# A nucleus-selection kernel whose repair branch sorts ties from real failures before it repeats

## What is computed

```python
Q = Xa @ W1; K = Xa @ W3
logits = Q @ W2 @ K.T / TAU
idx = jnp.argsort(-logits, axis=1)
vals = jnp.take_along_axis(logits, idx, axis=1)
csum = jnp.cumsum(jax.nn.softmax(vals, axis=1), axis=1)
k_i = jnp.sum(csum < P_NUC, axis=1) + 1          # P_NUC = 0.9
keep = jnp.take_along_axis(jnp.arange(n)[None, :] < k_i[:, None], jnp.argsort(idx, axis=1), axis=1)
A = jax.nn.softmax(jnp.where(keep, logits, -jnp.inf), axis=1)
...
for s in range(STEPS):                            # STEPS = 2
    A = _adj_from_feats(Xa, W1, W2, W3)
    Xf = Rf @ Xf; Xb = Rb @ Xb; Xa = A @ Xa
    Z = Z + (Xf @ U1[s] + Xb @ U2[s] + Xa @ U3[s])
```

## Time and profile before

| | us |
|---|---|
| median of 3 runs | 2081.41 |
| lowest, highest | 2080.66, 2081.58 |
| the execution that was profiled | 2080.55 |
| its span, first to last instruction | 2078.9 |
| mean granted TensorE clock | 0.951 of full speed |

### The profile page before, as it was taken

How to read it: one execution, slowest core, us unless ns; L and a number is a source line. 1 busy time by engine, 2 the same in 40 slices (tenths; PEclk the granted TensorE clock), 3 DMA queues, 4 the chain that set the end, 5 groups by cost and what they waited for, 6 DMA issues and landing times.

```text
span 2078.9 us, 37636 instructions
## 1 busy us (share of the span) xinstructions
PE 1784.7 (86%) x11660; PEld 1314.5 (63%) x11660; DVE 1667.7 (80%) x4213; ACT 1365.0 (66%) x2157; POOL 555.4 (27%) x869
## 2 busy tenths in 40 slices
PE   3999953899999999994765299999999999999997
PEld 2888831677777777773653166666666666666665
DVE  6444465899999999998851699999989999999996
ACT  5222266788888888884622586867676767677752
POOL 4000030343333333332230113131313232222220
PEclk9999976899999999997988699999999999999999
DMA  6999621444444444442333001010101010101022
GB/s 156 197 203 207 165 99 39 104 113 112 112 112 112 112 109 106 107 111 55 75 79 112 21 21 41 20 40 20 40 20 40 20 40 22 39 24 37 31 93 69
DMA packets 235346, 168.27 MB, mean 81 GB/s; under 512 B 188451, under 2 KB 220577, under 8 KB 235168
## 3 DMA queue, kind: packets, MB, share of 16 engines
q1 hardware_dynamic: 221264, 117.44, 20.8%
q0 software_dynamic: 3744, 22.14, 6.9%
q10 hardware_dynamic: 10288, 28.12, 4.0%
HBM read 107.99 MB, written 37.49 MB: 70 GB/s over the span
## 4 chain that ended last, share of the span: by engine, by line
DVE 46%; PE 18%; DVEq 17%; issue 11%; ACT 3%; DMA 3%; POOLq 0%; ACTq 0%; POOL 0%; SPq 0%
DVE probs_t L1508 7%; DVE stats L1525 5%; DVE stats L1515 5%; DVE window L1405 4%; DVEq L1706 4%; DVE scraps L1405 4%; DVE sorted_e L1534 2%; DVE window L1568 2%; DMA probs_t<-astray 2%; DVEq L1572 2%; DVE expo L1388 2%; DVEq L1532 2%; PE lg L1081 2%; PE bank L1029 2%; PE bank L1028 2%
## 5 line engine op out<-in xcount | busy, mean ns | idle before, releaser
L1081 PE MATMUL lg<-k_t,q_tile 64*128 64x512 f32 (+1 forms) x832 | 199.5, 582 | 134.3 <-DVE expo L1388 105.6
L1104 PE MATMUL bank<-both,s_tile 128*128 128x512 f16 x1352 | 300.1, 379 | 0.0
L1171 PE MATMUL bank<-xcur,probs_t 128*128 128x256 f32 x1352 | 296.1, 379 | 0.0
L1171 PEld LDWEIGHTS bank<-xcur,probs_t 128*128 128x128 f32 x1352 | 254.9, 190 | 33.6
L633 POOL TENSOR_TENSOR window<-window,probs_t 128x832 f16<-128x832 f32 x104 | 223.0, 2144 | 112.7 <-ACT probs_t L870 100.0
L1388 DVE TENSOR_SCALAR_CACHE_REDUCE expo<-lg 128x1024 f32 (+1 forms) x208 | 205.0, 1022 | 41.3 <-PE lg L1081 30.8
L1104 PEld LDWEIGHTS bank<-both,s_tile 128*128 128x128 bf16 x1352 | 132.3, 98 | 148.1
L1081 PEld LDWEIGHTS lg<-k_t,q_tile 64*128 64x128 f32 x832 | 72.2, 196 | 221.0 <-DVE expo L1388 134.3
L812 ACT ACTIVATE expo<-expo,neg_max 128x3327 f32<-128x3327 f32 x52 | 159.4, 3065 | 73.1 <-DVE neg_max L1397 73.1
L659 POOL TENSOR_TENSOR aims<-found 128x2 f32<-128x2 f32 x26 | 5.1, 194 | 649.0 <-ACT found L838 649.0
L833 ACT ACTIVATE turned<-expo,found 128x3327 uint8<-128x3327 f32 x52 | 159.7, 3071 | 3.6
(11 more groups left out here) (291 smaller groups left out, 3642.8 us busy)
## 6 DMA issues: line engine op xcount, KB each, us to landing
s_tile<-s_scratch SPq DMA_DIRECT2D x28, 832.0 KB, 4.5
expo<-in_adj POOLq DMA_DIRECT2D x25, 831.8 KB, 9.8
s_tile<-s_scratch ACTq DMA_DIRECT2D x24, 832.0 KB, 4.4
s_scratch<-s_tile SPq DMA_DIRECT2D x14, 832.0 KB, 9.8
s_scratch<-probs_t SPq DMA_DIRECT2D x6, 832.0 KB, 9.8
s_scratch<-window SPq DMA_DIRECT2D x6, 832.0 KB, 10.5
q_tile<-q_scratch SPq DMA_DIRECT2D x104, 32.0 KB, 2.1
xa_scratch<-ht ACTq DMA_DIRECT2D x26, 128.0 KB, 1.9
```

The lines of the kernel that those rows point to most:

```text
L1081: last = T.matmul(lg[c % 2][:, h * CHUNK:h * CHUNK + w], q_tile[b][DA * h:DA * (h + 1), :], k_all[DA * h:DA * (h + 1), s, c0:c0 + w], star ...
L1104: last = T.matmul(s_ps[:, 0:width], s_tile[b][:, k, :], moving, start=(k == 0 and part == 0), stop=(k == NT - 1 and part == 1))
L1171: last = T.matmul(kept_ps[1][:, 0:D], probs_t[:, k * P:(k + 1) * P], xcur[:, k, :], start=(k == 0), stop=(k == NT - 1))
```

## The change

Two things are done, both inside the repair branch.

First, in stage 0 alone, the test is taken again with ties allowed before the loop is entered: `tied` is taken out of `astray`, the list `equal` that `take_ties` needs is made, rows with more than 8 ties are put back, and `find_odd` and `reg_load` decide whether the loop runs at all. Secondly, in both stages, `take_ties` and `take_above` stand behind the loop, and are done once, instead of in each round.

```diff
                         dve.drain()
                         V.memset(tries, TRIES)
+                        if s == 0:
+                            V.tensor_tensor(astray[:, :], astray[:, :], tied, ALU.subtract)
+                            V.tensor_scalar(equal, ranks[:, :], tied, below[:, :], ALU.is_lt, ALU.mult)
+                            V.tensor_scalar(least, tied, 8.0, None, ALU.is_gt)
+                            dve.drain()
+                            V.tensor_tensor(astray[:, :], astray[:, :], least, ALU.add)
+                            dve.drain()
+                            find_odd(astray[:, :], t)
+                            dve.reg_load(left, odd_n[0:1, 0:1])
                         with dve.While(left):
                             move_cut(b)
                             rank(b)
                             flag(True)
                             dve.drain()
-                            take_ties(b)
-                            take_above(b, True, 0, N)
                             sum_kept()
                             find_odd(astray[:, :], t)
                             V.tensor_scalar(tries, tries, -1.0, None, ALU.add)
...
                             dve.reg_load(left, again)
+                        take_ties(b)
+                        take_above(b, True, 0, N)
+                        dve.drain()
                         dve.reg_load(left, odd_n[0:1, 0:1])
                         with dve.While(left):
                             climb(b)
```

## The result

The changed kernel took **2066.7 us** (median of 4 runs, 2066.2 to 2067.1) beside 2081.4 us of the kernel before on the same chip: a ratio of 0.993, 95% interval [0.9913, 0.9947]. So the change makes the kernel faster by 0.6 to 0.7%, 12 to 15 us. The forecast was 2068.8 us, 12.6 us less.

What follows compares the result with a forecast made beforehand. The prediction took DVE's two repair visits in stage 0 to lie on the path: -16.1 us in step 24 and +3.5 in step 22 make -12.6, from 2081.41 to 2068.8 us, range 2065.0 to 2074.5.

Steps and rivals of the forecast that it cites:

- What bounds it: Stage 0's repair branch, entered in steps 22 and 24, lies wholly on the path that sets the end.
- Which rows failed, and why: Step 22: row 1436's cut is too low, a true failure; step 24: row 1552 is only a tie.
- Rival 1: Step 24's row 1552 isn't a tie on the chip; the loop runs in both steps, +7.0 us, 2088.4 us; chance 0.05.
- rival 4: Both failures, steps 22 and 24, are ties, so 2 x 16.1 us go: 2049.2 us; chance 0.01.
- Step 24: Repair round skipped after the new test, masks kept; `kept_inv` at 1035.8 in place of 1051.89, 16.1 us earlier.
- Step 22: New test finds row 1436 and the loop runs: +3.2 us for the test, +0.3 for moved masks, +3.5 together.
- What is late next: After step 24's earlier `kept_inv`, ACT, POOL and PE still wait idle, margin 5.4 us on PE; gain passes in full.
- Rival 2: Step 24's gain is partly taken up in step 25 by a new wait, a third lost: 2074.2 us; chance 0.03.
- The sum: Whole kernel: -16.1 us in step 24 plus 3.5 in step 22 gives -12.6, so 2068.8 us.
- Stage 1 within 1 us: Sign to check: stage 1, untouched by the change, takes the same time as before to within 1 us.
- Rival 3: Stage 0's longer loop body makes each of 24 steps pay a 2.75 us jump, +66 us: 2134.8; chance 0.02.

Runs made afterwards that it cites:

- the cheaper test: Changed kernel with SyncE moving flag and `tied` per row and the entry test working on one partition instead of `find_odd`: 2066.4 us, ratio 0.9937; once more 2067.0.
- the filler runs: Changed kernel with 160, then 400 more instructions in the never-entered second loop of stage 0's repair branch: 2073.2 us (0.9967) and 2073.3 us (0.997).

## Why the prediction was right, point by point

- **What bounds it.** Both visits lie wholly on the path: a change of the branch's length by -27.5, +7.5 and +1.5 us in step 22, and by -27.4 and -15.3 us in step 24, came out at the end each time, within the spread of the runs. The -1.1 and -1.4 us of the cheaper test came as far as step 24's `kept_inv`, and are too small to be told apart at the end.
- **Which rows failed, and why.** Right in both, as far as it is shown: step 24 is entered for a tie alone, and step 22 for something other than a tie, by the two runs that leave out one kind of cause each. That it is the cut of row 1436 was worked out from the data, and no run shows it by itself. Rival 1 (2088.4) and rival 4 (2049.2) fall with it.
- **Step 24: -16.1 forecast, -15.28 measured.** Three terms were too small. From the MEMSET to L1670 it took 0.43 us (1028.06 - 1027.63) for 0.2 forecast; L1669 lasted 0.49 us here and 0.16 in step 22, and why is open. From `find_odd`'s last operation to L1565 it took 1.11 (1031.27 - 1030.16) for 0.21 + 0.31 + 0.3 = 0.82, since the jump over the skipped round is 0.49. From the mask's end, 1035.03 + 3.68 = 1038.71, to `kept_inv` it took 1.06 for 0.7: the jump over the second loop was 0.46, and the prediction had taken the 0.14 of the earlier trace rows. Together 0.9 us. The prediction had taken such jumps near the small end of 0.14 to 2.75 us, and that was the right end: they cost 0.5, none 2.75. But the filler runs show how near the other end lay: with a longer second loop the same jump is 2.7 us, and in the kernel with only the masks moved it is 0.14. The prediction had no reason by which to choose.
- **Step 22: +3.5 forecast, +2.89 measured.** The test took 2.74 for 3.2 (its first instructions came without a wait here), the moved masks 0.15 for 0.3.
- **What is late next.** Nothing, as forecast: ACT waits 12.92 for about 11.8, PE 9.90 for about 9. Rival 2 (2074.2) needed a new wait and there is none.
- **The sum.** -15.28 + 2.89 = -12.4 for -12.6. The two terms missed by 0.8 and 0.6 us in opposite directions, so that the sum is closer than its parts is luck. From step 21 to step 24 the four profiles give 135.39 and 135.99 before, 123.36 and 123.77 after: -12.1 us. The first measurement's 14.7 us hold some 2 us that are not the change's: 1.8 of the 13.7 in the profiles stand in stage 1, and the second profile of each kernel takes them back (there the whole difference is 10.5 us, with stage 1 being 1.1 us longer). "Stage 1 within 1 us" was too narrow by this chance; as a step of the argument it held.
- **Rival 3 (2134.8, each round pays a jump).** Wrong for this kernel and for one with a loop of 757 instructions. The Trainium skill (Runtime: NRT & Kernel Launch, Instruction fetch mechanics) says that an engine holds two blocks of 256 instructions and that a taken branch outside them forces a fetch. The trace disagrees for the rounds: a loop of 757 instructions, longer than two such blocks, shows 0.27 us at the jump over the branch and rounds no longer than before, where by that rule each round would have had a stall. It agrees for the entered branch, where the jump takes 2.7 to 3.0 us when the code it jumps over grows by 160 or 400.

## What to carry to other kernels

A repair branch that is entered twice in a kernel can be its dearest 55 us: count in the trace how often its lines ran, against the number of steps, and find for each entry which condition raised it before deciding what the entry must do. A flag that collects several causes should be split ahead of the expensive part, if the cheap causes don't need it; the split costs every true failure the test's own time (here 2.9 us against 15.3 gained). And compare the profiles of two executions of the same kernel before explaining a difference of 1 or 2 us that stands where the change has nothing.

## What the runs showed that I had not expected

- The granted clock of TensorE rises at another place of the same work from one execution to the next; all kernels here execute the same operations in stage 1, and in their 13 profiles it lasts from 967.4 to 969.7 us. Of the 2.5 us between the two spans of the changed kernel (2065.1 and 2067.6), 1.9 stand there.
- A visit of the branch that ends 27.5 us late costs 29.2 us: the other 1.8 (1.5 against the second profile of the kernel before) come two steps later, as a wait for a late transpose.
- Code that is never executed can have a price where a jump goes over it: 2.7 and 2.3 us for 160 instructions more, nothing more for 400, and nothing in the rounds of the loop, which jump over them each time. Each copy of the code was entered once here, so no run shows whether a second visit would pay again. Why the first jumps over the branch cost 2.75 us and the later ones 0.2 to 0.3, even in a loop of 757 instructions, stays open.
- The load of one register took 0.31 us each time, and the jump behind it 0.49 and 0.46 us in step 24 (the chain of work of the changed kernel; in the two kernels with only the masks moved and with the cheaper test the second is 0.14):

```profile
1030.37 0.31 DVEq L1676
1030.78 0.49 issue
...
1038.78 0.31 DVEq L1693
...
1039.17 0.46 issue
```
